# Two bf16 products of 512 and 256 columns behind each lone recurrence step

## The reference

```python
xn = _layernorm(x, g2, beta2)
U = (xn @ W_in.T + b_in) @ Bmat
def step(s, u_t):
    s = jax.nn.silu(s @ A.T) + u_t
    return (s, s)
_, states = jax.lax.scan(step, jnp.zeros((B, S), U.dtype), U.transpose(1, 0, 2))   # B = 4, S = 64
ssm_out = jnp.einsum('tbs,sh->bth', states, Cmat)
return residual + ssm_out + (program_probs.mean(axis=1) @ W_prog.T + b_prog)[:, None, :]
```

## Time and profile before

| | |
|---|---|
| median of 3 runs | 1563.16 us (1560.29 to 1566.49) |
| the profiled execution, its own time | 1560.21 us |
| its span, first to last instruction | 1558.4 us |
| mean granted TensorE clock | 0.959 |
| PE busy | 1373.5 us, 88% of the span |
| ACT busy, DVE busy | 1108.9 us (71%), 1061.6 us (68%) |
| lone steps, first load to last activation | 1471.3 to 1551.2 us |

### The profile page before, as it was taken

One profiled execution on the slowest core, in us unless ns is written; L12 is line 12 of the kernel. 1 busy time (PEld: TensorE's weight loads), 2 busy tenths in 40 slices (PEclk: granted clock), 3 DMA queues, 4 the chain that ended last, 5 costly groups with the idle time before them and its releaser, 6 DMA issues.

```text
span 1558.4 us, 36100 instructions
## 1 busy us (share of the span) xinstructions
PE 1373.5 (88%) x13434; PEld 1013.5 (65%) x13434; DVE 1061.6 (68%) x2383; ACT 1108.9 (71%) x3368; POOL 63.5 (4%) x119
## 2 busy tenths in 40 slices
PE   6899899997899889999978899997889999888855
PEld 5788656655566556677766667775666777666644
DVE  3766566765688778778777777877777787777400
ACT  3555688885677888777787767778877777877422
POOL 2100000000000000000000000000000000000000
PEclk9999999999999999999999999999999999999955
DMA  8322210003121113112101211210112121100100
GB/s 265 95 95 88 94 70 1 1 1 108 42 69 56 56 31 91 58 43 82 56 29 56 82 43 42 83 55 29 56 56 69 42 82 52 33 29 28 42 0 14
DMA packets 69596, 90.43 MB, mean 58 GB/s; under 512 B 5488, under 2 KB 58736, under 8 KB 69040
## 3 DMA queue, kind: packets, MB, share of 16 engines
q1 hardware_dynamic: 69312, 87.87, 17.7%
q0 software_dynamic: 112, 0.26, 0.1%
HBM read 71.33 MB, written 16.78 MB: 57 GB/s over the span
## 4 chain that ended last, share of the span: by engine, by line
PE 55%; ACT 21%; DVE 12%; issue 10%; DMA 1%; POOL 0%; ACTq 0%; DVEq 0%; SPq 0%; POOLq 0%
PE ps L1170 13%; PE ps L1473 11%; PE ps L1177 8%; PE ps L1184 6%; PE ps L1499 6%; ACT arena L698 5%; DVE arena L1119 4%; PE ps L1543 3%; ACT dAm L556 2%; PE ps L1243 2%; PE ps L1299 2%; PE ps L1458 2%; ACT R L758 1%; DVE nmax L1102 1%; ACT th L690 1%
## 5 line engine op out<-in xcount | busy, mean ns | idle before, releaser
L1170 PE MATMUL ps<-W,arena 128*128 128x128 f32 x2896 | 435.9, 284 | 29.5 <-ACT arena L698 21.2
L1170 PEld LDWEIGHTS ps<-W,arena 128*128 128x128 f32 x2896 | 325.0, 146 | 181.2 <-issue 132.5
L698 ACT ACTIVATE arena<-ps,nmax 128x512 f32<-128x512 f32 x640 | 434.6, 686 | 2.2 <-DVE nmax L1099 1.6
L705 ACT COPY arena<-ps 128x512 f32<-128x512 f32 x320 | 187.0, 584 | 215.4 <-PE ps L1170 211.2
L1099 DVE TENSOR_REDUCE nmax<-ps 128x1 f32<-128x512 f32 x320 | 206.1, 686 | 123.8 <-PE ps L1473 84.2
L1119 DVE COPY arena<-ps 128x512 f32<-128x512 f32 x320 | 213.8, 686 | 23.2 <-PE ps L1170 12.6
L1473 PE MATMUL ps<-W,arena 32*128 32x512 f32 x1280 | 186.8, 651 | 33.4 <-DVE arena L1119 32.7
L1499 PE MATMUL ps<-arena 128*32 128x128 f32 x5120 | 173.0, 276 | 31.2 <-ACT arena L705 31.0
L1102 DVE TENSOR_REDUCE nmax<-ps 128x2 f32<-128x1024 f32 x160 | 193.7, 1211 | 0.0
L1499 PEld LDWEIGHTS ps<-arena 128*32 128x32 f32 x5120 | 130.0, 109 | 69.1 <-ACT arena L705 58.7
L698 ACT ACTIVATION_READ_ACCUMULATOR arena<-ps,nmax 128x1 f32 x640 | 131.0, 205 | 0.0
(11 more groups left out here) (218 smaller groups left out, 1727.3 us busy)
## 6 DMA issues: line engine op xcount, KB each, us to landing
W<-keys SPq DMA_DIRECT2D x48, 512.0 KB, 3.7
arena<-values SPq DMA_DIRECT2D x48, 512.0 KB, 4.9
keys<-W SPq DMA_DIRECT2D x16, 448.0 KB, 3.3
values<-W SPq DMA_DIRECT2D x16, 448.0 KB, 3.9
W<-keys SPq DMA_DIRECT2D x16, 256.0 KB, 2.8
arena<-values SPq DMA_DIRECT2D x16, 256.0 KB, 3.3
W<-in_pack SPq DMA_DIRECT2D x1, 3180.0 KB, 10.4
W<-in_pack SPq DMA_DIRECT2D x1, 2246.0 KB, 10.8
```

What stands on the lines that cost most here:

```text
L698: nc.scalar.activation(Pr[:, a, :], ps[:, a, :], ACT.Exp, bias=nmax[:, u % 32:u % 32 + 1], accum_out=den[:, u % 32:u % 32 + 1]).then_inc(s ...
L705: nc.scalar.copy(PT[:, (4 * Q + a) % 8, :, :].rearrange("p k n -> p (k n)"), psT).then_inc(sem("u_ev_act"), 1)
L1170: ins = nc.tensor.transpose(dst[:, k * P:(k + 1) * P], src[:, k * P:(k + 1) * P], ident)
```

## The change

Behind each lone step's product TensorE issues two more. The weights are 64 columns of ones in bf16 on 64 partitions, the moving operand is 64 rows of `ones_b` with its 128 columns repeated 4 times and 2 times, and the results, 64 rows of 512 and of 256 columns, go to bank 6. Each starts its own sum. They have no semaphore, and nothing reads them.

```diff
@@ -1542,6 +1542,9 @@
                     pe.wait_ge(sem("e_r"), j)
                 mm(psR[0:S3, NB * j:NB * (j + 1)], W[0:S3, a3:a3 + S3], R2[0:S3, j, :], start=False, stop=True,
                    skip_group_check=True).then_inc(sem("e_z"), 1)
+                for n in (4, 2):
+                    mm(psX[1][0:S3, 0:n * P].rearrange("p (a n) -> p a n", a=n), ones_b[0:S3, 0:S3],
+                       ones_b[0:S3, :].unsqueeze(1).to_broadcast([S3, n, P]), start=True, stop=True)
             pe.wait_ge(sem("o_row"), (NCH - 1) * NB)
             pe.wait_ge(sem("e_half"), 2)
             for b in range(NB):
```

## The result

The changed kernel takes 1582.63 us (median of 4, 1578.83 to 1583.56), the kernel before beside it 1562.19 us (median of 4). The ratio is 1.0132, with a 95% interval of 1.0114 to 1.0151: 20.4 us slower. The profiled execution is the fastest of the four, 1578.83 us with a span of 1577.0 us.

The account below looks back on a forecast made before the run. Lone steps of product and activation at 1.2 GHz bound the tail; 122 steps costing 0.19 us more each add 23.6 us to 1560.2, giving 1584 us, or 1587 as a median. Own range 1580 to 1606; 8 in 10: 1546.5 to 1602.

Parts of the forecast that it names:

- The bound: Tail loop: each step's product and activation alternate alone on the path; 0.627 us a step at 1.2 GHz, 0.53 at 2.4.
- The stream at 2.4 GHz is hidden: Loop steps at 2.4 GHz: fillers end by 0.46 us, before the next step at 0.53, and cost nothing.
- The step at 1.2 GHz, 0.82 us: Loop steps at the lower clock: fillers aren't hidden, so the step grows by 0.19 us (0.14 to 0.38) from 0.627.
- The sum's term of 122 x 0.19 = 23.6 us: Loop steps after the clock falls: 122 of them cost 0.19 us more each.
- the rule on row groups: Filler loads: a load overlaps running matmuls only if its row group differs; would give 0.98 us a step, near 1606.
- the sum's 0.13 + 0.05: Step at 1.2 GHz: 0.13 us, under half of its two loads, plus 0.05 us for the filler's first load.
- The range by the step's bounds: Whole kernel: loop steps growing by 0.14 to 0.38 us, 122 times, add 17 to 47 us, 1580 to 1610 us.
- Which clock: Tail loop: whether the 64x64 fillers raise TensorE's clock; forecast that it falls where it does now; chance 0.52.
- the cells count: Clock in the loop: products count by array cells used, so a step's 768 columns are worth 192 of the full array.
- The argument from the narrow products that run four side by side: Stretches before the loop: four side by side did not hold the clock as four times the work would, so width counts.
- far less: Loop: by cells, six steps with fillers do far less work than either of the last two stretches compared for the clock.
- Rival 1: Tail loop and final products: fillers hold 2.4 GHz because streaming time counts; 13.5 us faster, 1550 us; chance 0.36.

Follow-up runs that it names:

- experiments 4: Kernel before plus, for each filler of 512 and 256 columns, four 64x64 products side by side on the array's quarters; 1548.34 us, ratio 0.9912.
- 5: Kernel before plus, for each filler, two 64x64 products side by side, on rows 0 to 63 and 64 to 127; 1549.20 us, ratio 0.9922.
- 6: Kernel before plus, for each filler, two 64x64 products side by side on rows 0 to 63, both column halves; 1548.64 us, ratio 0.9918.
- Experiments 2: Kernel before plus fillers of 512 and 256 columns on 128 rows and 64 columns of the array; 1562.71 us, ratio 1.0012.
- 3: Kernel before plus fillers of 512 and 256 columns on 64 rows and 128 columns of the array; 1615.40 us, ratio 1.0343.
- 10: Kernel before plus fillers of 512 and 256 columns on 128 rows and 32 columns of the array; 1562.02 us, ratio 0.9993.
- 12: Kernel before plus two 512-column fillers on 64x64 a step, doubled side by side in the first 16 steps; 1547.84 us, ratio 0.9916.
- experiment 1: Changed kernel with its fillers of 512 and 256 columns on 128x128 instead of 64x64; 1561.75 us, ratio 1.0001 against the kernel before.
- experiment 8: Kernel before plus one 512-column filler on 64x64 a step, without the changed kernel's 256-column one; 1560.55 us, ratio 0.9993.

## Why the prediction was right, and where it was not

The time, 1582.6 us for 1587, and the sign came out as forecast, and so did the low clock and the price of a step. The reason that I gave for the low clock was wrong, so that part of the outcome, on which the sign hangs, was in good part luck. Step by step:

- **The bound** (the lone steps alone on the path, all at 1.2 GHz but the first): right. The gains and losses that the traces above show lie in the loop and in the final products.
- **The stream at 2.4 GHz is hidden**: right. The changed kernel's first steps are 0.53 us apart, and in experiments 4 to 6 all are.
- **The step at 1.2 GHz, 0.82 us**: measured 0.80. The sum's term of 122 x 0.19 = 23.6 us is 122 x (0.800 - 0.627) = 21.1 us. The other loads run beside the stream as taken, so the rule on row groups (the Trainium skill, TensorE: Matmul & The Clock Gate, The mechanism), which would have made it 0.98 us, did not hold here: the product of step 1471.50 begins when the stream before it is through, 0.21 us after its own load, which lies beside that stream. The 0.02 us between 0.82 and 0.80 are in the stream: from the step's product to the fillers it is 0.18 us (1568.51 to 1568.69), which is the sum's 0.13 + 0.05, and from there to the next product 0.62 us rather than 0.64. The range by the step's bounds was 1580 to 1610; the prediction then names 1606 as its end, which no bound of the step gives. The measured time lies in both.
- **Which clock**: the outcome was right and the reason wrong. I wrote that the cells count. Experiments 2 and 3 (the same cells, different clocks) and 10 (the cells of the change, clock held) say that they don't. The fillers on 64x64 were too little because they feed only 64 of the 128 rows, at 768 columns a step: on all rows these 768 held the clock at widths of 128, 64 and 32 columns of the array, and on half of the rows twice the columns held it, 1024 went either way, and 768 lost it each time. The argument from the narrow products that run four side by side did not hold even by its own count: in cells, the stretch that lost the clock had 4 x 128 + 32 x 128 / 4 = 1536 columns of the full array and the one that kept it 12 x 128 = 1536, so a count by cells can't tell the two apart. Nor were six steps of the change "far less": 6 x 192 = 1152. Experiment 10 shows that a lone product of 32 columns' width on all rows holds the clock like one of 128.
- **Rival 1** (the fillers hold 2.4 GHz) was priced right at 13.5 us: experiments 4, 5, 6 and 12 gain 12.6 to 13.2 us over the kernel before. It needed more than the change has: fillers side by side, or longer ones. The rule behind it (the Trainium skill, TensorE: Matmul & The Clock Gate, What's actually happening: the clock follows how busy the engine has been) holds only with a measure of busy that the profile's busy column is not: PE is busy without a gap in the changed kernel and stays at 1.2 GHz.
- **Not foreseen**: that a filler of another shape than the step costs 0.10 to 0.12 us a step at 2.4 GHz. I named it in experiment 1 only, and too dear. The Trainium skill (TensorEngine Tiling (Array Packing), Key Properties) says that changing the tiling mode drains the engine; experiments 1, 2 and 10, with steps of 0.63 to 0.65 us at 2.4 GHz against 0.53 us for the same columns in the step's shape, agree with it.

**What stays open.** Two products side by side on the same 64 rows hold the clock (experiment 6). The records overlap, and 1536 columns one after another would take 0.64 us, more than the step of 0.53; but the runs don't say whether the second one counts by itself or only makes the stream last longer. If it counts by itself, one count puts all these kernels in order, the changed one too: rows fed times columns streamed, added up over the fillers of a step. I found it after the runs, none was made to test it, and it doesn't explain. Nor do the runs explain the fall behind 1385.4 us, where 32 narrow products ran four side by side on all rows: no experiment had four of that width. And experiment 12 was not run often enough to show that the start alone makes 1024 columns uncertain.

## What to carry to other kernels

A chain of short products that runs at TensorE's lower clock can be given the higher one by products that nobody reads, but they must be enough by the chip's measure and short enough to fit into the hole at the higher clock; if they miss the first, the same products stream at half the speed and no longer fit, so that the loss (20.4 us here) is larger than the gain would have been (13.5 us). Fillers short enough to fit at the lower clock too, as the 512 columns of experiment 8, cost nothing there, but did not raise the clock. Give fillers the shape of the products that they stand between, and put several of them side by side rather than one of another shape: here four of 64x64 gave 1548.3 us, and two of them 1549.2 and 1548.6 us, against 1561.8 us for one of 128x128, which covers the same cells as the four. Time such a kernel several times, since one at the edge comes out at either price.

## What the runs showed of the hardware that was not expected

- The granted clock stayed at 0.50 for 98 us in which PE's records left no gap. With the same 768 columns a step, a single product on all 128 rows held the clock at every width (128x128, 128x64, 128x32), and one on 64 rows lost it (64x64, 64x128).
- Two shapes in turn cost 0.10 to 0.12 us for a pair of changes at 2.4 GHz (steps of 0.63 to 0.65 us against 0.53). At 1.2 GHz it was more: the step of experiment 3 was 1.05 us, where the same columns in one shape take 0.80.
- A filler of the step's own shape starts to stream 0.14 us after the step's load, while the step's product is reported to end at 0.28 us. Only with another shape does it wait longer, 0.20 us.
